# Differences of sums inside second chunks, moved from VectorE's clamp to ScalarE's Relu

## What is computed

```python
cs = jnp.cumsum(dt * A, axis=-1)                 # one falling row per head, inside each chunk
seg = cs[..., :, None] - cs[..., None, :]        # 128 x 128 differences in each chunk
Lmat = jnp.where(tri, jnp.exp(seg), 0.0)
scores = jnp.einsum('bclhn,bcshn->bchls', Cc, Bc) * Lmat
Ydiag = jnp.einsum('bchls,bcshp->bclhp', scores, xdt)
```

## Time and profile before

| | |
|---|---|
| median of 3 runs | 2137.88 us (2137.7 to 2138.59) |
| the profiled execution: its time, its span | 2137.98 us, 2136.2 us |
| share of the span busy, PE / DVE / ACT / POOL | 98% / 78% / 65% / 31% |
| stages A, B and the first part of C | 0 to about 581 us |
| the 64 units of C | about 581 to 1910 us |
| end of C, and D | about 1910 to 2136 us |

### The profile page before, as it was taken

One profiled execution on the slowest core, in us unless ns is written; L12 is line 12 of the kernel. 1 busy time (PEld: TensorE's weight loads), 2 busy tenths in 40 slices (PEclk: granted clock), 3 DMA queues, 4 the chain that ended last, 5 costly groups with the idle time before them and its releaser, 6 DMA issues. The chain is left out here.

```text
span 2136.2 us, 35778 instructions
## 1 busy us (share of the span) xinstructions
PE 2083.9 (98%) x10641; PEld 1669.7 (78%) x10641; DVE 1672.2 (78%) x2922; ACT 1385.5 (65%) x2744; POOL 672.2 (31%) x416
## 2 busy tenths in 40 slices
PE   9999999989989999999999999999999999998998
PEld 7888778867867787878777777878778777877876
DVE  7655446458888888888888888888888888878875
ACT  3222125433488888879888888888878888863232
POOL 6644334311113324233333324233333323330010
PEclk9999999999999999999999999999999999999999
DMA  5312404222332222232222223232332322212432
GB/s 196 110 56 91 163 1 133 74 51 95 118 138 100 92 101 99 69 124 69 98 95 98 98 84 108 70 113 74 103 113 70 108 85 99 76 48 84 143 98 80
DMA packets 63887, 204.31 MB, mean 96 GB/s; under 512 B 14960, under 2 KB 15216, under 8 KB 55184
## 3 DMA queue, kind: packets, MB, share of 16 engines
q1 hardware_dynamic: 63760, 202.97, 27.7%
HBM read 194.04 MB, written 8.91 MB: 95 GB/s over the span
## 5 line engine op out<-in xcount | busy, mean ns | idle before, releaser
L72 PE MATMUL bank<-xT_hi,C_w_hi 128*128 128x512 f32 x1160 | 474.6, 409 | 6.5 <-POOL C_w_lo L1746 2.5
L73 PE MATMUL bank<-xT_lo,C_w_hi 128*128 128x512 f32 x1160 | 461.8, 398 | 0.0
L74 PE MATMUL bank<-xT_hi,C_w_lo 128*128 128x512 f32 x1160 | 461.1, 398 | 0.0
L1719 POOL TENSOR_TENSOR C_w_lo<-C_raw,C_w_hi 128x512 fp32r<-128x512 f32 x130 | 168.7, 1298 | 862.2 <-ACT C_w_hi L1816 798.8
L1411 DVE SCALAR_TENSOR_TENSOR C_acc<-bank,C_par,C_acc 128x510 f32<-128x510 f32 (+2 forms) x384 | 282.6, 746 | 93.6 <-ACT C_acc L1771 70.3
L1517 DVE TENSOR_TENSOR C_decay<-C_decay,C_cb 128x512 f32<-128x512 f32 x384 | 265.4, 719 | 40.8 <-ACT C_decay L1913 36.3
L72 PEld LDWEIGHTS bank<-xT_hi,C_w_hi 128*128 128x128 f32 x1160 | 219.9, 190 | 64.6 <-issue 11.4
L74 PEld LDWEIGHTS bank<-xT_hi,C_w_lo 128*128 128x128 f32 x1160 | 219.5, 189 | 53.3
L73 PEld LDWEIGHTS bank<-xT_lo,C_w_hi 128*128 128x128 f32 x1160 | 219.8, 190 | 47.0
L72 PE MATMUL bank<-C_out_hi,C_yg_hi 128*128 128x512 f32 x512 | 200.8, 392 | 5.0 <-DVE C_yg_lo L1487 4.7
L74 PE MATMUL bank<-C_out_hi,C_yg_lo 128*128 128x512 f32 x512 | 200.0, 391 | 0.0
(11 more groups left out here) (280 smaller groups left out, 4288.6 us busy)
## 6 DMA issues: line engine op xcount, KB each, us to landing
C_cs_row<-cs_rows SPq DMA_DIRECT2D x64, 1024.0 KB, 5.4
C_raw<-in_Cxg SPq DMA_DIRECT2D x65, 512.0 KB, 3.6
ahead_raw<-in_D SPq DMA_DIRECT2D x32, 512.0 KB, 3.6
C_raw_out<-in_Cout SPq DMA_DIRECT2D x64, 256.0 KB, 2.9
front_raw<-in_A SPq DMA_DIRECT2D x20, 512.0 KB, 4.3
B_stat_raw<-in_D SPq DMA_DIRECT2D x16, 512.0 KB, 3.6
cb_rows<-C_decay SPq DMA_DIRECT2D x8, 768.0 KB, 3.3
C_cb<-cb_rows SPq DMA_DIRECT2D x8, 768.0 KB, 4.4
```

The source lines that it names most:

```text
L72: pe.matmul(out, lh, rh, start=start, stop=False)
L73: pe.matmul(out, lh, rl, start=False, stop=False)
L74: return pe.matmul(out, ll, rh, start=False, stop=stop)
L1719: e.tensor_tensor(w_lo[:, slot, :], raw_at, f32(w_hi[:, slot, :]), ALU.subtract).then_inc(lo_done, 1)
```

## The change

VectorE's `clamp` is gone. A new `ease_second(u, h)` on ScalarE writes the same four tiles of round 4 + h as a Relu of scalar minus row, so with the other sign, and `second_exp` takes it with scale -1. In all units but the first both calls stand behind `y_high(u,0)` and ahead of `root` and `decay_exp`; in the first unit they stand behind `gate_weights`, ahead of `second_exp`. VectorE's two waits in `clamp` for the rows and for the matmuls go with it (and two more in the first unit); ScalarE gets no other wait.

```diff
--- before.py
+++ after.py
@@ -1516,20 +1516,6 @@
                 e = decay[:, r, :]
                 v.tensor_tensor(e, e, cb[:, r % 2 if r < 4 else 2, :], ALU.mult).then_inc(S.m_done, 1)
 
-            def clamp(u, h):
-
-                if h == 0:
-                    v.wait_ge(cs_in[u.j], (u.U - u.j) * 8 + 16)
-                    wait(v, S.y_mm, u.U * 2)
-                    if u.first:
-                        v.wait_ge(S.cb_stored0, 8 * GROUPS)
-                        v.wait_ge(S.cb_stored1, 8 * GROUPS)
-                for b in range(BATCH):
-                    t = slice(P * b, P * (b + 1))
-                    v.tensor_scalar(decay[:, 4 + h, t], cs_row[:, u.j, N * h + SEQ * b + CHUNK:N * h + SEQ * (b + 1)],
-                                    cs_t[:, 2 * b + 1, bass.ds(u.U * 2 + h, 1)], 0.0, ALU.subtract, ALU.min)\
-                     .then_inc(S.clamped, 1)
-
             def x_steps(u, h):
                 v.wait_ge(S.x_turned, u.U * 2 + (h + 1))
                 wait(v, S.y_mm, u.U * 2)
@@ -1643,8 +1629,6 @@
                     if u.group_ended:
                         mean_square(u, g)
                     y_low(u.V, 1 - s, 0)
-                clamp(u, 0)
-                clamp(u, 1)
                 if u.first_pair and u.j == 1:
                     quantised(0)
                     quantised(1)
@@ -1898,6 +1882,13 @@
                     a.activation(first_of(u, h, b), cs_row[:, u.j, at:at + CHUNK], ACT.Relu, scale=-1.0,
                                  bias=cs_t[:, 2 * b, bass.ds(u.U * 2 + h, 1)]).then_inc(S.eased, 1)
 
+            def ease_second(u, h):
+
+                for b in range(BATCH):
+                    at = N * h + SEQ * b + CHUNK
+                    a.activation(decay[:, 4 + h, P * b:P * (b + 1)], cs_row[:, u.j, at:at + CHUNK], ACT.Relu, scale=-1.0,
+                                 bias=cs_t[:, 2 * b + 1, bass.ds(u.U * 2 + h, 1)]).then_inc(S.clamped, 1)
+
             def decay_exp(u):
 
                 for h in range(2):
@@ -1916,7 +1907,7 @@
 
                 for h in range(2):
                     a.wait_ge(S.clamped, u.U * 8 + (4 * h + 4))
-                    a.activation(decay[:, 4 + h, :], decay[:, 4 + h, :], ACT.Exp).then_inc(S.decays, 1)
+                    a.activation(decay[:, 4 + h, :], decay[:, 4 + h, :], ACT.Exp, scale=-1.0).then_inc(S.decays, 1)
 
             def root(g):
                 a.wait_ge(S.ms_done, g)
@@ -1946,6 +1937,8 @@
                     x_silu(u, 1)
                     ease(u, 1)
                     y_high(u, 0)
+                    ease_second(u, 0)
+                    ease_second(u, 1)
                 if u.group_ended:
                     root(u.g)
                 decay_exp(u)
```

## The result

The changed kernel takes 2242.06 us (median of 4, 2238.67 to 2244.64) against 2137.79 us: a ratio of 1.0488, 95% interval 1.0472 to 1.0504, so 104 us slower, 6 us less than forecast. The profiled execution has a span of 2240.2 us, 104.0 more than before, and the comparison of the traces is between these two.

A forecast was written before the change was run, and what follows sets the result against it. TensorE bounds C before, a ScalarE-VectorE loop after: 62 rounds with eight Relus, `group_scaled`, `root` and jumps give +107.0 us, start +1.3, tail +1.5, in all +109.8 on 2137.98: about 2248 us, 8 in 10 for 2222 to 2265.

The forecast's parts named there:

- The forecast sum: Predicted time from the first tap of unit 1 to that of unit 63: 1394.9 us, against 1287.9 before, +107.0 us.
- The loop: ScalarE-VectorE round in C, tap to next tap: 19.13 us (j = 0) and 19.94 (j = 1), becoming 21.49 and 22.30.
- unit 40: Unit behind the outer loop's jump where ScalarE, not TensorE, is late; the loop's length, 19.13 us, was read there.
- `group_scaled`: Extra ScalarE work in seven units of C, 2.22 us each, 15.5 us in the sum.
- `root`: Extra ScalarE work in seven units of C, 1.52 us each, 10.6 us in the sum.
- the jumps: Six outer-loop jumps where ScalarE waits for no one the profile shows: 2.08 us less 0.19 each, 11.3 us in all.
- the likeliest case: The forecast itself, the bound moving from TensorE to the ScalarE-VectorE loop: about 2248 us, given 78%.
- Start +1.3: Ahead of unit 1, ScalarE's 1.07 us of idle takes up some of the 2.36 us of Relus: +1.3 us.
- tail +1.5: Behind unit 63, where tap to table load goes from 9.18 us to 8.30 + 2.36: +1.5 us.
- By occupancy: First rival: ScalarE's 3.1 us idle a unit in C covers the Relus, TensorE stays the bound, 2135 to 2138 us; 4%.
- The second rival: In C only ScalarE's waits for TensorE, 2.15 us a unit, are slack, but all of them: 2154 us; 5%.
- The clock rival: TensorE's new gaps of nearly 2 us at `out_tile(u,0)` in every second unit lower its clock: about 2260 us; 12%.

The follow-up runs named there:

- the relief alone: The kernel before without clamps and without the new Relus, leaving out the differences inside second chunks: 2136.64 us, ratio 0.9999.
- the reordered kernel: Changed kernel with ScalarE's `ease` calls each ahead of their `x_silu` and four of the eight new Relus ahead of `y_high(u,0)`: 2215.55 us, ratio 1.0370.
- the cost alone: The kernel before, clamps kept on VectorE, plus eight Relus a unit on ScalarE into a tile nobody reads: 2240.69 us, ratio 1.0486.
- the kernel with the late Relus: Changed kernel with the eight Relus moved from ahead of `decay_exp` to behind it, straight ahead of `second_exp`: 2272.43 us, ratio 1.0626.

## Why the prediction was right, point by point

- *TensorE bounds C before, VectorE and ScalarE have room.* Right: without any clamp the kernel takes the same time, and two Relus a unit are hidden in most rounds. TensorE's need was read 0.1 us too low: the 40.82 us were a stretch without a gap and not a pair of units. From the first matmul of one `inside` (1349.89 us) to that two units on (1390.90) it is 41.01, so 20.5 us a unit. The forecast sum doesn't use it.
- *VectorE's relief is worth nothing; it waits longer for the Exps.* Right: its wait is 4.6 us where I said some 3, and neither the relief alone nor the clamps kept beside the Relus moved the time. VectorE was to be hidden with 0.5 us to spare; in unit 38 it is idle for 0.43 us ahead of the next convolution.
- *Eight Relus cost 2.36 us.* In the trace 2.45 us from the first to the table load behind (1437.52 - 1435.07). But from the first tap to the table load it is 10.64 us where I had 8.30 + 2.36 = 10.66.
- *The loop, 21.49 and 22.30 us.* 21.46 and 22.12. The odd round was mis-sized by 0.18: I took the 8.30 us of unit 40 up to the table load for all units, and in odd units it is 10.49 - 2.36 = 8.13, since ScalarE waits 1.53 and not 1.71 us for the convolution (unit 37). Thirty-one rounds at 0.17 are 5 us.
- *`group_scaled`, `root`, the jumps.* The jump wait came out as 2.1 us in the mean (line 1755 waits 12.4 us for "issue", six times, between 800 and 1890 us) and is paid in full now. `group_scaled` was put at 2.22 us and costs 2.08: seven such units take 23.54 and not 23.71 us, 1 us less in sum. Units 41, 49 and 57 cost 1 us more each by the clock, for which the likeliest case had nothing. Less 5 and less 1, and 3 more, lead from 1394.9 to within 0.2 us of the measured 1391.7. So errors of both signs partly cancel, but none is larger than 5 of 107 us: the hit isn't luck.
- *Start +1.3, tail +1.5.* Unit 0 does take 20.17 instead of 18.87 us, 1.3 more as forecast, but its first tap began 1.3 us earlier (580.20 against 581.51), in work that the change doesn't touch; over the traces of all runs it begins anywhere from 578.91 to 583.17 us. Behind unit 63 TensorE starts `inside` 21.18 us behind the first tap and not 19.88, 1.3 us later where 1.5 were forecast; yet the rest of the run was 1.1 us shorter. Both terms are there, and the span doesn't show them, because what one execution varies by elsewhere is as large.
- *Rivals.* By occupancy the time would have stayed at 2138 us. The result speaks against it, and the reordered kernel against reading occupancy alone: same work, 27 us less. (The loop was 1.5 us too long for that rival, not 1.4.) The Trainium skill (Perfetto Trace Analysis, "Optimizing Scalar/DVE Operations") lets work go to ScalarE where VectorE is saturated; VectorE was 87% busy here, and without the clamps the time stayed the same, so that premise doesn't hold and no run here tests the advice where it does. The second rival, waits for VectorE that don't grow, fell with the 86.1 us, 28.6 before. The clock rival's mechanism is there behind the longest gaps (2.7 us and more), but its price is some 3 or 4 us and not 12, and filling the gaps gained nothing that whole runs can show: in the ordinary rounds the gaps were 1.4 us, shorter than the 2 us that I took, and no drop followed. A granted clock below 1 in the middle of C was named as a sign of being wrong, and it came, 0.98 in the stretch; it was the sign of this small term and not of another mechanism.

## What to carry to other kernels

Before work goes to an engine with idle time, find a round in which that engine is the late one, and read there which of its idle time is left. Of ScalarE's 3.1 us a unit here the profile before put 2.15 down to waits for TensorE, and still only 0.7 could be used: a unit got 103.8 / 62 = 1.67 us longer by 2.36 us of Relus. As ScalarE got later, waits for the answer of the very engine that was to be relieved took the place of those for TensorE, 2.1 us in unit 38. Then test the cost alone and the relief alone; here the one gave all of the loss and the other no gain. Slack is also local: a loop that is short enough in the mean costs time in the rounds where it isn't.

## What the runs showed of the hardware that I had not expected

A VectorE instruction with two operands in SBUF (`y_low`, 128x512) takes 0.74 us by itself and 2.70 us when it starts 0.26 us behind a POOL sum of 128x1024; with POOL's sum cut to 128 columns it takes 0.76 us at the same place. In the kernel with the late Relus all 26 that start behind POOL's sum take 2.66 to 2.93 us, and each ends 0.55 us behind POOL's instruction, as if it had stood until POOL was done. Started 0.15 us ahead of POOL's sum, as in the changed kernel (1448.12 and 1448.27 us), it isn't stretched; there POOL's sum takes 2.82 us and not 2.40. The kernel before has the collision too, in units 9, 17 and so on to 57: `y_low` starts 0.13 us behind POOL's 1.37 us subtraction for `out_lo` and takes 1.78 us. So which of the two starts first decides which is held up, and an engine that gets done earlier can run into an instruction of another that it used to miss.
